# A bidirectional Mamba layer on one core: ScalarE's list reordered, clipping on VectorE, softplus without Relu, prologue by halves

## What is computed

```python
xz = einsum('ed,bld->bel', in_proj_w, xn)        # 256 channels x, 256 channels z
out_f = mamba_dir(xz, ...)                       # forward
out_b = mamba_dir(xz[:, :, ::-1], ...)[:, :, ::-1]   # backward, own weights
y = einsum('bdl,od->blo', out_f + out_b, out_proj_w)
result = x + y + ffn(xn)

# mamba_dir: u = silu(conv4(x) + b); x_dbl = xproj @ u -> dt (8 rows), B (16), C (16)
# delta = softplus(dt_w @ dt + dt_bias);  dA = exp(delta * A);  dBx = delta * B * u
# h[l] = dA[l] * h[l-1] + dBx[l]  for 256 channels x 16 states;  y = sum_n h * C + D * u;  y * silu(z)
# ffn: Hadamard transform of xn, 4-bit quantization by token (round, clip to -8..7, rescale), ternary weight
```

## Time and profile before

| | us |
|---|---|
| median of 3 runs (lowest to highest) | 982.82 (979.82 to 986.75) |
| the profiled execution | 989.38 |
| its span, first to last instruction | 987.6 |
| busy in the span: TensorE, VectorE, ScalarE, GpSimd | 802.9, 787.0, 780.7, 788.1 |
| mean granted TensorE clock | 0.875 |
| length of inner batches, four windows in a row | 116.05 each |

### The profile page before, as it was taken

How to read it: one execution, slowest core, us unless ns; L and a number is a source line. 1 busy time by engine, 2 the same in 40 slices (tenths; PEclk the granted TensorE clock), 3 DMA queues, 4 the chain that set the end, 5 groups by cost and what they waited for, 6 DMA issues and landing times.

```text
span 987.6 us, 13840 instructions
## 1 busy us (share of the span) xinstructions
PE 802.9 (81%) x3873; PEld 381.5 (39%) x3873; DVE 787.0 (80%) x795; ACT 780.7 (79%) x1452; POOL 788.1 (80%) x493
## 2 busy tenths in 40 slices
PE   2478887979888897888889797897978889797974
PEld 1134434343443434333353434434343343434352
DVE  2248887988888888888789887888978887988982
ACT  2469896988959887798869889698887988699950
POOL 1038978997899887898789977989879897798994
PEclk9677998899998989889879989889898898898796
DMA  3070607051160605215070421607043150704300
GB/s 86 11 162 29 135 4 182 3 123 41 57 136 3 159 3 124 68 53 107 3 170 24 115 44 39 154 3 159 3 104 88 33 129 3 169 15 99 61 22 11
DMA packets 50841, 72.44 MB, mean 73 GB/s; under 512 B 6128, under 2 KB 19328, under 8 KB 50816
## 3 DMA queue, kind: packets, MB, share of 16 engines
q1 hardware_dynamic: 50384, 71.87, 31.3%
q10 hardware_dynamic: 432, 0.26, 0.1%
HBM read 60.58 MB, written 11.53 MB: 73 GB/s over the span
## 4 chain that ended last, share of the span: by engine, by line
POOL 33%; issue 32%; ACT 13%; PE 11%; DVE 7%; SPq 1%; DMA 1%; POOLq 1%; DVEq 0%; ACTq 0%
POOL hst L612 22%; ACT da L370 5%; POOL dbx_t L622 5%; DVE hst L512 4%; PE pb L744 3%; ACT dbx_t L359 3%; POOL t_log L628 3%; PE b_ps L827 2%; PE b_ps L824 2%; POOL xn L674 2%; DVE b_ps L500 1%; PE pb L751 1%; PE y L841 1%; DMA rep<-d_scr 1%; PE pb L771 1%
## 5 line engine op out<-in xcount | busy, mean ns | idle before, releaser
L612 POOL TENSOR_TENSOR hst<-hst,c_rep 128x1024 f32<-128x1024 f32 x256 | 601.4, 2365 | 132.2 <-DVE hst L512 128.4
L512 DVE TENSOR_TENSOR_SCAN hst<-da,b_ps 128x512 f32<-128x512 f32 x512 | 589.5, 1203 | 82.1 <-ACT da L370 43.4
L827 PE MATMUL b_ps<-ident,dbx_t 128*128 128x128 f32 x1536 | 241.9, 298 | 127.3 <-DVE hst L512 120.1
L370 ACT ACTIVATE da<-rep,neg_a 128x511 f32<-128x511 f32 x512 | 335.6, 709 | 6.4 <-DMA rep<-d_scr 6.3
L827 PEld LDWEIGHTS b_ps<-ident,dbx_t 128*128 128x128 f32 x1536 | 178.2, 150 | 277.5 <-DVE hst L512 230.1
L359 ACT ACTIVATE dbx_t<-du_t,b_t 128x256 f32<-128x256 f32 x576 | 248.1, 495 | 2.9 <-PE b_ps L827 2.9
L841 PE MATMUL y<-hst,sum_sel 128*32 128x512 f32 x1024 | 166.6, 730 | 0.0
L744 PE MATMUL pb<-xnt,conv_wt 128*128 128x512 f32 x256 | 120.7, 616 | 0.7 <-ACT xnt L291 0.7
L824 PE MATMUL b_ps<-t_log,spread_sel 32*128 32x512 f32 x256 | 89.3, 698 | 10.6 <-DVE hst L512 10.6
L500 DVE TENSOR_TENSOR b_ps<-b_ps,b_rep 128x1024 f32<-128x1024 f32 x64 | 78.1, 1220 | 21.6 <-PE b_ps L824 21.6
L622 POOL TENSOR_TENSOR dbx_t<-du_t,b_t 128x1024 f32<-128x1024 f32 x48 | 91.2, 1901 | 2.7 <-ACT du_t L342 2.7
(11 more groups left out here) (90 smaller groups left out, 598.5 us busy)
## 6 DMA issues: line engine op xcount, KB each, us to landing
rep<-d_scr SPq DMA_DIRECT2D x128, 256.0 KB, 9.3
c_rep<-bc_scr SPq DMA_DIRECT2D x64, 256.0 KB, 5.0
d_scr<-t_pos SPq DMA_DIRECT2D x16, 512.0 KB, 3.0
b_rep<-bc_scr SPq DMA_DIRECT2D x64, 64.0 KB, 2.4
x_ln<-x SPq DMA_DIRECT2D x8, 256.0 KB, 3.2
x_res<-x SPq DMA_DIRECT2D x8, 256.0 KB, 2.9
out<-x_res SPq DMA_DIRECT2D x8, 256.0 KB, 9.5
conv_wt<-conv_w SPq DMA_DIRECT2D x2, 512.0 KB, 5.9
```

What stands on the lines that cost most here:

```text
L370: nc.scalar.activation(da[s % 2][:, j, 1:L], rep[d][h][:, j, 1:L], ACT.Exp, scale=neg_a[:, d, h, j, q:q + 1]).then_inc(decay_done, 1)
L512: nc.vector.tensor_tensor_scan(hst[s % RING][:, j, :], da[s % 2][:, j, :], b_ps[:, j, :], 0.0, ALU.mult, ALU.add).then_inc(scan_done, 1)
L612: nc.gpsimd.tensor_tensor(hst[s % RING][:, two, :], hst[s % RING][:, two, :], c_rep[d][:, q:q + 1, :].broadcast_to([P, 2, L]), ALU.mult).t ...
L827: ins = tr(b_ps[:, j, P * c:P * (c + 1)], dbx_t[(NX * d + q - 1) % 2][:, c, NJ * h + j, :, :].rearrange("p r e -> p (r e)"), ident[:, :])
```

## The change

- **ScalarE's list.** The unit's loop is written anew. `inputs_t` parts move (the first of q = 1 stands at the end of slot 7, the others one step later than before, the parts of q = 3 in slots 4 and 5), `u_sigmoid` 0 and 1 go from the two halves of slot 0 to the end of slot 0 and the middle of slot 1, `keep_xdbl` and `keep_xqt` from the end of slot 1 to the middle of slot 2, `keep_bt` from the middle of slot 2 to its end, `guess_rstd` behind the decays that follow the log, `z_sigmoid` to the end of slot 5, `normalize` from slot 4 to 6, `keep_longer` from 4 to 6, `keep_xnt` and the forward unit's `keep_dut` from 6 to 7. In a backward unit the first `keep_dut` goes to the end of slot 7 and the second into the next unit's slot 0, behind its first decays. GpSimd's `refine` goes from slot 3 to 4.
- **Clipping.** GpSimd's `clip` and `rescale` go; `quantize` on VectorE does them (one pass over 128x512 in PSUM, four of 128x128 out of it).
- **Softplus.** The bias of the step comes in as a row of `dtw` against a row of ones in `xdbl` (made by the bias of `keep_xdbl`); the Relu pass goes, and the last VectorE pass takes max(., 0) of the step in PSUM. 1 + exp is written to `t_pos` instead of `pb`, and the correction works there.
- **Product with B.** `times_b` is issued one step before its scan instead of directly before it.
- **TensorE.** Both convs of the forward unit stand in slot 7, as those of the backward unit do.
- **Prologue.** Layer norm's instructions come before the exponential of A; conv before the transpose of the ternary weight; the steps before the product that transposes B; softplus, delta, its store and its load, and delta*u by halves; `b_rep` and `c_rep` are loaded before delta is ready.

```diff
             def quantize(b):
...
                 for c in range(NC):
-                    ins = nc.vector.tensor_scalar(xq[:, c, :], pb[:, 0, P * c:P * (c + 1)], qinv[:, c:c + 1], ROUND, ALU.mult, ALU.add)
-                ins.then_inc(had_read, 1)
+                    at = slice(P * c, P * (c + 1))
+                    ins = nc.vector.tensor_scalar(pb[:, 0, at], pb[:, 0, at], qinv[:, c:c + 1], ROUND, ALU.mult, ALU.add)
+                ins.then_inc(xq_step, 1)
+                dve.wait_ge(xq_step, 2 * b + 1)
+                nc.vector.tensor_scalar(pb[:, 0, :], pb[:, 0, :], ROUND, Q_POS, ALU.subtract, ALU.min).then_inc(xq_step, 1)
+                dve.wait_ge(xq_step, 2 * b + 2)
+                for c in range(NC):
+                    ins = nc.vector.tensor_scalar(xq[:, c, :], pb[:, 0, P * c:P * (c + 1)], -Q_NEG, qscale[:, c:c + 1], ALU.max, ALU.mult)
+                ins.then_inc(xq_ready, 1)
...
             def delta(V):
                 dve.wait_ge(cor_step, 2 * V + 2)
-                nc.vector.tensor_tensor(t_pos[:, :, :], t_pos[:, :, :], pb[:, :, :], ALU.subtract).then_inc(delta_ready, 1)
+                nc.vector.scalar_tensor_tensor(t_pos[:, :, :], pb[:, :, :], 0.0, t_pos[:, :, :], ALU.max, ALU.subtract).then_inc(delta_ready, 1)
...
                 for s in range(SLOTS):
+                    if s == 0:
+                        times_b(b, d, 0, 0)
                     scan(b, d, s, 0)
+                    if s < NH:
+                        times_b(b, d, s, 1)
...
                     scan(b, d, s, 1)
+                    if s < NH - 1:
+                        times_b(b, d, s + 1, 0)
```

The prologue on ScalarE, and SyncE's part of it:

```diff
-            act.wait_ge(w_loaded, DMA * W_LOADS)
-            nc.scalar.activation(neg_a[:, :, :, :, :], neg_a[:, :, :, :, :], ACT.Exp).then_inc(a_exp, 1)
             log_var(0)
             guess_rstd(0)
             normalize(0)
             keep_xnt(0)
+            act.wait_ge(w_loaded, DMA * W_LOADS)
+            nc.scalar.activation(neg_a[:, :, :, :, :], neg_a[:, :, :, :, :], ACT.Exp).then_inc(a_exp, 1)
...
-            spread(0, 0)
+                sp.dma_start(dtw[d][ONE:ONE + 1, :], dt_bias[d:d + 1, :]).then_inc(w_loaded, DMA)
+            store_bc(0, 0)
+            load_bc(0, 0)
+            sp.wait_ge(first_delta, 1)
+            sp.dma_start(d_scr[0][0], t_pos[:, 0, :]).then_inc(first_stored, DMA)
+            sp.wait_ge(first_stored, DMA)
+            load_delta(0, 0)
+            sp.wait_ge(delta_ready, 1)
+            sp.dma_start(d_scr[0][1], t_pos[:, 1, :]).then_inc(delta_stored, DMA)
+            sp.wait_ge(delta_stored, DMA)
+            load_delta(0, 1)
```

More of the change, by code:

```diff
@@ L28 @@
 XC = 64
+ONE = DR + 2 * NS
 RING = 4
@@ L32, with build @@
 NX = NQ - 1
-def build(nc, x, win_t, wz_t, conv_w, cols, xproj_t, dt_t, a_log, wout_t, ffn_w, had, ident_d, sum_sel_d, spread_d, out):
+def build(nc, x, win_t, wz_t, conv_w, cols, xproj_t, dt_t, dt_bias, a_log, wout_t, ffn_w, had, ident_d, sum_sel_d, spread_d, out):
     ctx = ExitStack()
@@ L322, in softplus_in, with softplus_log @@
+            def softplus_log(V):
+                act.wait_ge(sp_step, 4 * V + 2)
+                nc.scalar.activation(t_exp[:, :, :], t_exp[:, :, :], ACT.Exp, scale=-1.0).then_inc(sp_step, 1)
+                act.wait_ge(sp_step, 4 * V + 3)
                 wait(act, delta_stored, DMA * V)
                 wait(act, du_ready, V)
-                for n, h in enumerate((1, 0)):
-                    act.wait_ge(dt_filled, 2 * V + n + 1)
-                    nc.scalar.activation(t_exp[:, h, :], pb[:, h, :], ACT.Abs, bias=col[:, d, 1, h:h + 1]).then_inc(sp_step, 1)
-                    nc.scalar.activation(t_pos[:, h, :], pb[:, h, :], ACT.Relu, bias=col[:, d, 1, h:h + 1]).then_inc(sp_step, 1)
@@ L417, in unit @@
                             log_var(b + 1)
-                            guess_rstd(b + 1)
-                    if s == 5 and d == 0:
-                        z_sigmoid(b)
-                    if s == 6 and d == 0:
+                    if s in (4, 5):
+                        inputs_t(d, U, 3, 2 * (s - 4))
+                    if s == 6 and d == 0 and not last(b):
+                        normalize(b + 1)
+                    if s == 7 and d == 0:
                         if not last(b):
@@ L710, in unit @@
                         inputs_t(e, 1)
-                    if s == 7 and d == 1:
-                        clip(b)
-                        clipped(b)
                     if s == 5 and d == 1:
@@ L718, in unit @@
                         scales(b)
-                    if s == 7 and d == 1:
-                        rescale(b)
                     if d == 0 and not last(b):
@@ L810, in project, with copies @@
                     ins.then_inc(out_filled, 1)
+            def copies(S, h, p):
+                for j in (2 * p, 2 * p + 1):
+                    at = slice(CB * j, CB * (j + 1))
+                    wait(pe, scan_done, NJ * (S - 1) + j + 1)
+                    mm(b_ps[:, j, :], spread_sel[at, :], du[at, h, :], start=True, stop=True).then_inc(t_filled, 1)
             def inputs(b, d, s, p):
@@ L816, in inputs @@
                     pe.wait_ge(du_ready, 2 * b + d + 1)
-                elif h == 0 and p == 0:
+                    copies(S, h, p)
+                    return
+                if h == 0 and p == 0:
                     pe.wait_ge(bm_act, NX * (2 * b + d) + q)
@@ L847, in _ @@
             transpose_xn(0, xn_ready, 1)
+            pe.wait_ge(weights_ready, 2)
+            pe.wait_ge(xnt_ready, 1)
+            conv(0, 0, 0, range(TAPS), xnt_ready, 1)
+            conv(0, 0, 1, range(TAPS), xnt_ready, 1)
             pe.wait_ge(fw_ready, 1)
-            tr(pb[:, 1, 0:DM], ft, ident[:, :]).then_inc(fwt_filled, 1)
+            tr(y[:, 0, 0:DM], ft, ident[:, :]).then_inc(fwt_filled, 1)
             pe.wait_ge(w_loaded, DMA * W_LOADS)
             pe.wait_ge(weights_ready, 5)
-            pe.wait_ge(xnt_ready, 1)
-            conv(0, 0, 0, range(TAPS), fwt_read, 1)
-            conv(0, 0, 1, range(TAPS), xnt_ready, 1)
             x_proj(0, 0)
-            b_transposed(0, 0, u_ready, 2)
+            steps(0, 0, xdbl_ready, 1)
             steps(0, 1, xdbl_ready, 1)
-            steps(0, 0, bt_ready, 1)
+            for c in range(NC):
+                ins = mm(y[:, 1, NS * c:NS * (c + 1)], xdbl[0][0:XC, P * c:P * (c + 1)], ident[0:XC, DR:DR + NS], start=True, stop=True)
+            ins.then_inc(bt_filled, 1)
+            pe.wait_ge(first_du, 1)
+            copies(0, 0, 0)
+            copies(0, 0, 1)
             du_transposed(0, 0, delta_ready, 1)
@@ L925, in unit @@
                         if d == 1:
-                            du_transposed(V, 1, had_read, b + 1)
-                        elif not last(b):
-                            pe.wait_ge(xnt_ready, b + 2)
-                            conv(d, U + 2, 0, range(TAPS), dut_ready, 2 * V + 1)
-                    if s == 7 and d == 1 and not last(b):
+                            du_transposed(V, 1, xq_ready, b + 1)
+                    if s == 7 and not last(b):
                         conv(d, U + 2, 1, range(TAPS), dut_ready, 2 * V + 2)
@@ L975 @@
         "conv_w": np.stack([v[s[0]][:, 0, :].T for s in sides]),
[L976 removed]
+        "cols": np.stack([np.stack([halves(v[s[n]]) for n in (1, 6)], 1) for s in sides], 1),
         "xproj_t": np.stack([halves(v[s[2]].T) for s in sides]),
         "dt_t": np.stack([v[s[3]].T for s in sides]),
+        "dt_bias": np.stack([v[s[4]] for s in sides]),
         "a_log": np.stack([v[s[5]].reshape(NH, NJ, CB, NQ, NR).transpose(4, 2, 0, 1, 3).reshape(P, NH, NJ, NQ) for s in sides], 1),
```

194 lines of the change are left out of this document (106 added, 88 removed).

## The result

The changed kernel takes 999.96 us (996.43 to 1002.61) beside 981.32 (978.13 to 986.75) before: a ratio of 1.0182, with an interval of 1.0121 to 1.0243. It is slower by 1.2 to 2.4%, where 928 us and a clear gain were forecast. The profiled execution took 1002.61 us, its span is 1000.8.

What follows compares the result with a forecast made beforehand. No engine was taken as the bound: each idles about 18 us of a 116.05 us batch. Prologue -13.2, six inner batches -30.3, first -3.5, last -3, tail -4.5 sum to -54.5, so 928 us; range 895 to 958.

Steps and rivals of the forecast that it cites:

- Clipping: Clip and rescale moved onto VectorE, ahead of a scan: +1.75 us per batch, bounds 1.2 and 2.2.
- ScalarE's order: ScalarE's reordered list in the batches: 5.9 of 6.9 us of VectorE's decay waits gone per batch, bounds 0 to 6.9.
- Relu, Abs and the logs: Softplus in the batches: Relu's removal takes 2.3 us per batch off ScalarE, the maximum costs VectorE nothing, no table load added.
- The prediction's own sign of being wrong: Inner batch staying above 114 us, then look at waits for bt and xn's copy; or first decays after 55 us.
- TensorE's 4.3 us: VectorE's wait per batch for injected inputs from TensorE, taken as unchanged: 0, bounds -3 to +4.
- The first rival: In the batches, TensorE's and the log's waits fall too and VectorE becomes the bound: 103 us per batch, 869 us; chance 0.2.
- The product with B: VectorE's product issued one step ahead of its scan: waits on its own instruction shrink from 1.3 to 0.3 us, -1.0 per batch.
- The scale's wait: VectorE's 1.5 us wait per batch for the quantization scale from GpSimd, taken as unchanged: 0, bounds -1.5 to +0.5.
- The prologue: Start of the run: first decays at 49.7 instead of 62.9 us, -13.2 us, bounds -8.3 to -15.
- The tail: End of the run: GpSimd's clip and rescale and some transpose time go, later scans cost 1.75: -4.5 us.
- half clock in the dense stretch: Rival for slots 7 to 1: TensorE's low clock loses 4.5 us in each of 16 units, giving 1000 us; chance 0.04.
- VectorE becomes the bound: Rival for the batches: TensorE's and the log's waits fall too, a batch takes 103 us, the kernel 869; chance 0.2.

Runs made afterwards that it cites:

- the slowest (1020 us): The kernel before with only 1 + exp written to an SBUF tile instead of PSUM, so both correction passes read two SBUF operands: 1020.26 us, ratio 1.0372.

## Why the prediction was wrong

By the runs the change can be put together step by step. Each step is the difference of two medians, and each holds only in this order:

| step | us | to | forecast |
|---|---|---|---|
| before | | about 982.5 | |
| prologue | -11 | 971.6 | -13.2 |
| bias by a row | -7.5 | 964.0 | 0 |
| ScalarE's order, conv's place | -9.1 | 954.9 | about -40 in the batches |
| product sooner | -12.8 | 942.1 | about -7 |
| clipping on VectorE | +13.7 | 955.9 | +12, less 4.5 for the tail |
| no Relu, correction in SBUF | +44.1 | 1000.0 | 0 |

**The step that failed** is in "Relu, Abs and the logs": "VectorE takes the maximum with 0 inside the last correction pass, which it ran already, so that costs nothing (bounds 0 to 0.1 us per pass, as PSUM and SBUF operands change places)". The pass that takes the maximum did cost nothing (1.19 us). But the raw step has to stay in PSUM for it, so the two passes ahead of it lost their PSUM operand, and they went from 1.22 and 1.23 to 1.89 and 2.99 us. The bound was drawn from passes with one operand in PSUM. The kernel before has large passes with two SBUF inputs only in its prologue (`conv_wt<-conv_wt,hst`, 1.22 us each), and no GpSimd pass ran beside them, so they were no slower than the rest. A bound would have had to come from GpSimd's side: a product of 2.37 us that can hold VectorE once for each pass. That gives up to 4.7 us per unit and a top end of about 71 us for the 15 units. The range held nothing like it, and none of the rivals named it. The prediction's own sign of being wrong, a batch above 114, was met; but bt and the copy of xn, where it said to look, are not what VectorE or ScalarE waits for in that batch.

**ScalarE's order** was right in its mechanism and wrong in what it is worth. The decay waits fell as forecast, to 0.8 us in the batch. But between the kernels with and without the new order (964.0 and 954.9 us) the whole-run waits moved rather than went: decays 39.4 to 7.2 and log 28.8 to 12.5, against transposed inputs from TensorE (L827 before) 14.2 to 38.3 and u 11.0 to 32.2. That is 48.5 us off and 45.3 on. The step was "I leave TensorE's 4.3 us as it is: 0 (bounds -3 to +4)": behind the decays the next in line was TensorE. The wait for u comes at all 32 u, behind the two convs. The convs aren't all of it: one wait for transposed inputs, 2.36 us at slot 3 of a middle batch, stands behind TensorE's steps and sums at the lower clock (two matmuls at 404.15 take 2.07 us, two at 400.61 1.10). The first rival asked what would be late next, and the forecast didn't.

**The product with B** was forecast at -1.0 a batch. Own waits fell to 0.7 us a batch, but the move gave -12.8, +18.3 or +12.2 us depending on the list it stood in, and the sign went with TensorE's clock behind the wait for u. The prediction's condition, that the TensorE matmul must be there sooner too, was the one that failed: the product's wait for it rose from 0.8 to 6.3 us a batch.

**Clipping** was sized right on VectorE (1.9 us a batch against 1.75: busy 96.97 without it and 98.91 with it) and too low in what it holds up: a batch grew by 2.9 us even without the slow passes. **The scale's wait** was 1.0 instead of 1.5, within its bounds. **The prologue** was 1.4 us short: first decays at 51.16 instead of 49.7, from a first half of delta done at 41.67 instead of 39.6, with the way through memory 0.6 quicker than reckoned. Part of the delay is the same contention from the other side. Layer norm stands earlier now, and its small GpSimd steps, 0.20 us each in the earlier trace rows, meet that product of conv_wt with two SBUF inputs:

```profile
8.64 2.36 DVE L583 TENSOR_TENSOR conv_wt<-conv_wt,hst 128x1024 f32<-128x1024 f32 x2 [3.33 <-DMA conv_wt<-conv_w]
8.91 1.01 POOL L714 TENSOR_TENSOR shift<-rstd 128x4 f32<-128x4 f32 x1 [1.83 <-ACT rstd L303]
9.88 1.18 POOL L715 TENSOR_TENSOR var<-var,const 128x4 f32<-128x4 f32 x1
```

They take 1.8 us longer together, on the path to normalizing. **The tail** gave 6.4 from the last scan on, where the forecast had 6.1 (its 4.5 takes 1.75 off for later scans). That the rival "half clock in the dense stretch" names 1000 us is luck: the passes alone make 38 us in the kernel before, and it has nothing of them; with softplus as before and the same convs in slot 7 the kernel takes 956 us at a mean granted clock of 0.894. A grain of it is there: x_proj, in that stretch, took over 2 us in 14 of 15 units after and in 7 before, but 0.8 to 1.7 us over its 1.93 and not 4.5, and the mean clock was 0.865 and 0.875. "VectorE becomes the bound" had the right engine in part: it is the busiest now, at 103.6 us of 119.4, but by becoming slower, and it still stands idle for 16 us of a batch.

So with softplus as before the change gives 956 us, 2.9% off and not the 5.6% forecast; without Relu it is 1.8% slower than the kernel before. Two steps failed, then: the passes, which turned the sign, and the worth of ScalarE's order, which would have left the gain at half its forecast anyway.

## What to carry to other kernels

When an edit frees an instruction by leaving a value where it lies, ask which other instructions lose that place: here one pass less on an engine with idle time pushed two passes of the busiest engine from PSUM to SBUF, beside GpSimd, which reads SBUF and is busy for 77% of the span. Look in the groups by shape for a mean that grew at the same element count, since such waiting counts as busy and stands in no list of waits. And when a wait is taken away, price the batch by the next wait in line and not by the one removed; after reordering three engines' lists only runs of the combinations told what each edit was worth. Where an edit gains in one list and loses in another, compare the granted clock and the mean of the same matmuls before explaining it by waits.

## What was not expected of the hardware

A VectorE pass with two SBUF inputs (128x1024) takes 1.3 to 3.3 us in the batches of the changed kernel, beside GpSimd's products, where the same pass with one PSUM operand takes 1.23 and one with two SBUF inputs and GpSimd idle 1.22; on half the size, 0.69 alone and 1.63 beside GpSimd. GpSimd's own pass beside it goes from 1.90 to 2.88. The granted clock of the profiled runs was highest, 0.904, in the fastest kernel (942 us) and lowest, 0.861, in the slowest (1020 us). And behind the same 2.00 us of idle time the same four matmuls took 1.93 us at full clock in one kernel and 3.25 at a granted 0.57 in another; inside one kernel a batch with one slower x_proj was some 2.2 us longer (109.2 and 111.4, and 113.2 and 115.5).
